# Transformer block on eight cores: LayerNorm sums on ScalarE, four broadcast buffers, seven probability buffers, output stored in halves

## The reference

```python
x = x + attn(_layernorm(x), ...)
x = x + ffn(_layernorm(x), ...)

# attn: 16 query heads of 64, one K and one V head for all
q = jnp.einsum('bnd,hkd->bnhk', r, query_proj)
k = jnp.einsum('bmd,dk->bmk', r, key_proj)
v = jnp.einsum('bmd,dv->bmv', r, value_proj)
sim = jnp.einsum('bnhk,bmk->bnhm', q, k) / jnp.sqrt(64)
o = jnp.einsum('bnhm,bmv->bnhv', softmax(sim), v)
out = jnp.einsum('bnhv,dhv->bnd', o, output_proj)

# ffn: 64 channels, an inner width of 16 for each
s = jnp.einsum('btd,dm->btm', x, Win) + bin_
h = relu(s[..., None] * W1 + b1)
g = jnp.einsum('btmh,mh->btm', h, W2) + b2
out = jnp.einsum('btm,md->btd', g, Wout) + bout
```

## Time and profile before

| | us |
|---|---|
| median of 2 runs | 1667.75 (1655.49 to 1680.01) |
| the profiled execution | 1658.1 |
| its span, slowest core (core 4) | 1656.5 |
| spans of the eight cores | 1645.0 to 1656.5 |
| TensorE busy | 1099.0 (66%) |
| ScalarE busy | 1043.5 (63%) |
| VectorE busy | 472.7 (29%) |
| GpSimd busy | 94.9 (6%) |

### The profile page before, as it was taken

One profiled execution on the slowest core, in us unless ns is written; L12 is line 12 of the kernel. 1 busy time (PEld: TensorE's weight loads), 2 busy tenths in 40 slices (PEclk: granted clock), 3 DMA queues, 4 the chain that ended last, 5 costly groups with the idle time before them and its releaser, 6 DMA issues.

```text
span 1656.5 us, 20837 instructions; the slowest of 8 cores (1645.0 to 1656.5 us)
## 1 busy us (share of the span) xinstructions
PE 1099.0 (66%) x7407; PEld 419.4 (25%) x7424; DVE 472.7 (29%) x759; ACT 1043.5 (63%) x1203; POOL 94.9 (6%) x188
## 2 busy tenths in 40 slices
PE   0366534899999698999789999799997225152420
PEld 0233222333333233333233333233332002020110
DVE  1655676100101110101210101110102036453643
ACT  0211121899999799999799999799998001120201
POOL 0000000000000010000100100100100010000000
PEclk9977755899999899999899999899999658585755
DMA  6211121300000200000200000200000322234232
GB/s 168 101 53 53 53 103 43 104 1 1 1 1 2 66 17 9 12 14 3 66 17 9 16 10 3 66 17 9 17 10 3 116 68 95 84 119 140 78 138 89
DMA packets 27924, 81.75 MB, mean 49 GB/s; under 512 B 9008, under 2 KB 10032, under 8 KB 27568
## 3 DMA queue, kind: packets, MB, share of 16 engines
q1 hardware_dynamic: 19120, 60.87, 11.1%
q0 software_dynamic: 8704, 19.54, 3.6%
HBM read 60.34 MB, written 25.17 MB: 52 GB/s over the span
## 4 chain that ended last, share of the span: by engine, by line
ACT 36%; PE 18%; DMA 17%; DVE 15%; issue 12%; SPq 1%; DVEq 0%; POOLq 0%; ACTq 0%
ACT ptu L496 35%; DMA rcpb<-zscr 4%; DMA zscr<-zscr 4%; DMA big<-x2d 3%; PE qps L334 3%; DMA x2d<-big 3%; PE spa L481 2%; PE oBe L520 2%; PE oAe L520 2%; DVE stats L193 2%; PE spb L481 2%; PE kps L307 2%; DVE g L649 1%; DVE big L676 1%; DVE big L671 1%
## 5 line engine op out<-in xcount | busy, mean ns | idle before, releaser
L496 ACT ACTIVATE ptu<-spb 128x1024 bf16<-128x1024 f32 x512 | 568.5, 1110 | 32.3 <-PE spb L481 31.7
L496 ACT ACTIVATE ptu<-spa 128x1024 bf16<-128x1024 f32 x512 | 569.6, 1112 | 1.5 <-PE spa L481 1.5
L520 PE MATMUL oBo<-ptu,vab 64*65 64x512 bf16 x1024 | 389.8, 381 | 31.7 <-DVE big L535 29.2
L520 PE MATMUL oAo<-ptu,vab 64*65 64x512 bf16 x1024 | 388.5, 380 | 2.5 <-DVE big L535 0.5
L520 PE MATMUL oBe<-ptu,vab 64*65 64x512 bf16 x1024 | 387.3, 378 | 1.4
L520 PE MATMUL oAe<-ptu,vab 64*65 64x512 bf16 x1024 | 385.3, 376 | 1.7
L481 PE MATMUL spb<-qt,k2t 64*128 64x512 bf16 x1024 | 211.5, 384 | 39.0 <-ACT ptu L496 0.9
L481 PE MATMUL spa<-qt,k2t 64*128 64x512 bf16 x1024 | 205.4, 383 | 48.0 <-ACT ptu L496 6.1
L204 ACT ACTIVATE stats<-stats,epsb 128x1 f32<-128x1 f32 x48 | 14.1, 295 | 352.7 <-DVE stats L202 352.7
L535 DVE COPY big<-oBo 65x512 f32<-65x512 f32 x32 | 22.0, 687 | 660.1 <-PE oBo L520 659.8
L222 PE MATMUL trpsA<-identb,r1u 128*128 128x128 bf16 x256 | 32.0, 303 | 165.6 <-DVE r1u L212 165.6
(11 more groups left out here) (60 smaller groups left out, 824.9 us busy)
## 6 DMA issues: line engine op xcount, KB each, us to landing
xbuf<-x_own SPq DMA_DIRECT2D x32, 512.0 KB, 3.3
xbuf<-x_oth SPq DMA_DIRECT2D x16, 512.0 KB, 3.2
rcpb<-zscr POOLq DMA_DIRECT2D x64, 128.0 KB, 2.6
x2d<-big POOLq DMA_DIRECT2D x16, 512.0 KB, 2.9
big<-x2d SPq DMA_DIRECT2D x16, 512.0 KB, 4.2
out<-big SPq DMA_DIRECT2D x16, 512.0 KB, 3.0
xbuf<-wq SPq DMA_DIRECT2D x8, 512.0 KB, 4.5
xbuf<-wp SPq DMA_DIRECT2D x8, 512.0 KB, 4.0
```

The source lines that it names most:

```text
L496: expT[gmc] = S.emit("scalar", lambda s_, gmc=gmc: s_.activation(ptu[:, gmc % 8, :], sp[gmc % 2][:], AF.Exp, scale=0.125), waits=ew, inc=" ...
L520: tgt = S.emit("tensor", lambda te, ob=ob, rg=rg, col=col, mc=mc, gmc=gmc: te.matmul(ob[:], vab[rg:rg + 64, mc, :], ptu[rg:rg + 64, gmc % ...
```

## The change

Five edits.

1. LayerNorm sums, in both parts: `ln_stage1` gives Square an accumulator output for the sum of squares, and adds an Identity activation with an accumulator output for the sum. Both reductions of VectorE go.
2. `rcpb` has four buffers instead of two; each has a semaphore of its own (`zs`, `zs2`, `zs3`, `zs4`). A multiply waits for its own broadcast, a broadcast no longer for the one in front, and four are issued ahead.
3. `ptu` has seven buffers instead of eight (one buffer is 2 KB of each partition, what the two new buffers of `rcpb` take is 4 KB). Exponential `gmc` now waits for `pvT[gmc - 4]` too. `pvT` is set by the matmul with `oi == 3`, the last of the four in a pass, and for gmc-4 that is pass gmc-2.
4. In `emit_D` the reload of tile t waits for the spill of tile t instead of the newest spill, and for the first of the two adds of tile t-2 instead of the second.
5. The output of a tile is stored as two halves of 512 columns by two DMAs with two semaphores.

```diff
-        rcpb = st.enter_context(nc.sbuf_tensor("rcpb", [128, 2, NTW], F32))
+        rcpb = st.enter_context(nc.sbuf_tensor("rcpb", [128, 4, NTW], F32))
-        ptu = st.enter_context(nc.sbuf_tensor("ptu", [128, 8, 1024], BF16))
+        ptu = st.enter_context(nc.sbuf_tensor("ptu", [128, 7, 1024], BF16))
...
         def ln_stage1(li, xt_ap, sc, sq_waits=()):
             dmp = dump(li % 2)
             ln_state["sqa" + str(li)] = S.emit(
-                "scalar", lambda s, a=xt_ap, dmp=dmp: s.activation(dmp, a, AF.Square),
-                waits=list(sq_waits) + [("dve", ln_state["sq2"].get(li - 1, 0))], inc="act")
+                "scalar", lambda s, a=xt_ap, dmp=dmp, c=sc: s.activation(
+                    dmp, a, AF.Square, accum_out=stat(SUMSQ, c)),
+                waits=list(sq_waits) + [("act", ln_state["sq"].get(li - 1, 0))], inc="act")
             ln_state["sq"][li] = S.emit(
-                "vector", lambda v, a=xt_ap, c=sc: v.reduce_sum(stat(SUMS, c), a, axis=AX),
-                waits=[w for w in sq_waits if w[0] != "act"], inc="dve")
+                "scalar", lambda s, a=xt_ap, dmp=dmp, c=sc: s.activation(
+                    dmp, a, AF.Identity, accum_out=stat(SUMS, c)),
+                waits=[("act", ln_state["sqa" + str(li)])], inc="act")
 
         def ln_stage2(li, sc):
-            dmp = dump(li % 2)
-            tsq2 = S.emit("vector", lambda v, c=sc, dmp=dmp: v.reduce_sum(stat(SUMSQ, c), dmp, axis=AX),
-                          waits=[("act", ln_state["sqa" + str(li)])], inc="dve")
-            ln_state["sq2"][li] = tsq2
             S.emit("vector", lambda v, c=sc: v.tensor_scalar_mul(stat(EX2, c), stat(SUMSQ, c), 1.0 / D),
-                   waits=[("dve", tsq2)])
+                   waits=[("act", ln_state["sq"][li])])
...
-            zw = zst["bcT"][max(zst["bcT"])]
-            mw = [("zs", zw), ("dve", tcopyT[k * NHP + i_ // 2])]
+            mw = [(ZS[i_ % 4], zst["bcT"][i_]), ("dve", tcopyT[k * NHP + i_ // 2])]
...
-            if i_ + 2 < HEADS:
-                emit_bcast_ref[0](k, i_ + 2)
+            if i_ + 4 < HEADS:
+                emit_bcast_ref[0](k, i_ + 4)
...
-                ew = [("pe", sPT[gmc])]
+                ew = [("pe", sPT[gmc]), ("pe", pvT.get(gmc - 4, 0))]
...
-                    ptu[:, gmc % 8, :], sp[gmc % 2][:], AF.Exp, scale=0.125),
+                    ptu[:, gmc % 7, :], sp[gmc % 2][:], AF.Exp, scale=0.125),
...
-                            if zst["bcT"]:
-                                bw.append(("zs", zst["bcT"][max(zst["bcT"])]))
-                            if i_ >= 2:
-                                bw.append(("dve", multT[(kk, i_ - 2)]))
+                            if i_ >= 4:
+                                bw.append(("dve", multT[(kk, i_ - 4)]))
...
-                        for i_ in range(2):
+                        for i_ in range(4):
                             emit_bcast(k, i_)
...
-                xw = [("g", spill_t[max(spill_t)]), ("dve", fadd_t.get(t - 2, 0)),
+                xw = [("g", spill_t[t]), ("dve", tfa_t.get(t - 2, 0)),
                       ("dve", multT.get((KL, HEADS - 1), 0))]
...
-                outdma_t[t] = S.emit("sync", lambda e, t=t, q=q: e.dma_start(
-                    out_d.rearrange("(t p) d -> t p d", p=128)[t], obuf(q)),
-                    waits=[("dve", fadd_t[t])], inc=osem, inc_n=16)
+                for h in range(2):
+                    outdma_t[(t, h)] = S.emit("sync", lambda e, t=t, q=q, h=h: e.dma_start(
+                        out_r[t, :, h * 512:(h + 1) * 512], obuf(q)[:, h * 512:(h + 1) * 512]),
+                        waits=[("dve", fadd_t[t])] if h == 0 else (), inc=osems[h], inc_n=16)
```

More of the change, by code:

```diff
@@ L25 @@
 ENGS = ("sync", "tensor", "vector", "scalar", "gpsimd")
-SEMS = ("pe", "dve", "act", "xa", "xb", "xc", "xd", "g", "zg", "zs", "out", "ou2", "wd", "od", "zh", "pl", "x2r")
+SEMS = ("pe", "dve", "act", "xa", "xb", "xc", "xd", "g", "zg", "zs", "zs2", "zs3", "zs4", "out", "ou2", "ou3", "ou4", "wd", "od", "zh", "pl", "x2r")
 DMA_SEMS = {"xa", "xb", "g", "zg", "zs", "out"}
@@ L448, in emit_zmult @@
                 odma_fin[k] = zst["odmaT"]
+        ZS = ("zs", "zs2", "zs3", "zs4")
         emit_bcast_ref = [None]
@@ L520, in build_nc @@
                 tgt = S.emit("tensor", lambda te, ob=ob, rg=rg, col=col, mc=mc, gmc=gmc: te.matmul(
-                    ob[:], vab[rg:rg + 64, mc, :], ptu[rg:rg + 64, gmc % 8, col:col + 512],
+                    ob[:], vab[rg:rg + 64, mc, :], ptu[rg:rg + 64, gmc % 7, col:col + 512],
                     start=(mc == 0), stop=(mc == MC - 1)),
@@ L564, in build_nc @@
                         if k > 0 and (k - 1) in zstate:
-                            rw.append(("zs", zstate[k - 1]["bcT"][15]))
-                            tzw.append(("zs", zstate[k - 1]["bcT"][15]))
+                            for s_ in range(4):
+                                rw.append((ZS[s_], zstate[k - 1]["bcT"][12 + s_]))
+                                tzw.append((ZS[s_], zstate[k - 1]["bcT"][12 + s_]))
                         trec = S.emit("vector", lambda v: v.reciprocal(recipz[:], zstage[:]),
@@ L583, in emit_bcast @@
                             bw = [("zh", tzo)]
[L584 to L587 removed]
+                            if i_ >= 4:
+                                bw.append(("dve", multT[(kk, i_ - 4)]))
                             else:
[L589 removed]
+                                bw.append(("dve", multT.get((kk - 1, 12 + i_), 0)))
                             zst["bcT"][i_] = S.emit("gpsimd", lambda e, i_=i_: e.dma_start(
[L591 removed]
+                                rcpb[0:64, i_ % 4, :],
                                 zscr.rearrange("c h n -> h c n")[i_]),
[L593 removed]
+                                waits=bw, inc=ZS[i_ % 4], inc_n=16)
                         emit_bcast_ref[0] = emit_bcast
[L596 removed]
+                        for i_ in range(4):
                             emit_bcast(k, i_)
@@ L619, in build_nc @@
         r2evac_t = {}
+        tfa_t = {}
+        out_r = out_d.rearrange("(t p) d -> t p d", p=128)
         spill_t = {}
@@ L664, in emit_D @@
                 sm = "wd" if t % 2 == 0 else "x2r"
-                osem = "out" if t % 2 == 0 else "ou2"
-                xw = [("g", spill_t[max(spill_t)]), ("dve", fadd_t.get(t - 2, 0)),
+                osems = ("out", "ou3") if t % 2 == 0 else ("ou2", "ou4")
+                xw = [("g", spill_t[t]), ("dve", tfa_t.get(t - 2, 0)),
                       ("dve", multT.get((KL, HEADS - 1), 0))]
@@ L672, in emit_D @@
                     obuf(q), x2dbuf(q), fo[:], op=ALU.add),
-                    waits=[("pe", fo_mm_t[t]), (sm, txl), (osem, outdma_t.get(t - 2, 0)),
+                    waits=[("pe", fo_mm_t[t]), (sm, txl),
+                           (osems[0], outdma_t.get((t - 2, 0), 0)),
+                           (osems[1], outdma_t.get((t - 2, 1), 0)),
                            ("dve", multT.get((KL, HEADS - 1), 0))],
                     inc="dve")
+                tfa_t[t] = tfa
                 fadd_t[t] = S.emit("vector", lambda v, q=q: v.tensor_tensor(
@@ L761, in build_nc @@
                 waits=S.barrier_waits("gpsimd"), inc="g", inc_n=16)
-        S.emit("gpsimd", lambda e: e.nop(), waits=[("out", outdma_t[14]), ("ou2", outdma_t[15])])
+        S.emit("gpsimd", lambda e: e.nop(), waits=[
+            ("out", outdma_t[(14, 0)]), ("ou3", outdma_t[(14, 1)]),
+            ("ou2", outdma_t[(15, 0)]), ("ou4", outdma_t[(15, 1)])])
         S.flush()
```

2 lines of the change are left out of this document (1 added, 1 removed).

## The result

The changed kernel takes 1695.9 us (median of 9 runs, 1691.5 to 1697.4), the kernel before 1656.95 (median of 8 runs). The ratio is 1.0237, with a 95% interval of 1.0223 to 1.0251: slower. The forecast was 1701, within 1664 to 1738. Ratios leave out runs in a slower state, in which the cores of one die show a lower granted clock (1677 at 0.75 instead of 0.86 in one run of the kernel before); here these are two of the eight before, 1679 and 1680.

A forecast was written before the change was run, and what follows sets the result against it. ScalarE's exponentials were taken to set attention's pace, a chain of short waits the last part's. First part -29, attention +113, last part -41 give +43 on a span of 1656.5; with 1.6 around it 1701 us, range 1664 to 1738.

The forecast's parts named there:

- The exponential's wait: Attention: exponentials wait for the pass's last PV matmul, 2.10 us for two instead of 1.83; +147 before the stalls' 34 go.
- The boundary's 0.5 a head pair: Attention, between head pairs: TensorE's remaining stall on PSUM copies adds 0.5 us a pair, making 34.1.
- The three stalls: Attention, near the start of query tiles 1 to 3: ScalarE stalls of about 11.3 us each go, 34 in all.
- First part: LayerNorm of 32 tiles with K, V, Q products: a tile step falls from 4.46 to 3.9 us, -29 in all.
- the ring that was argued: First part: Ln waits for VectorE's small operations, these for the Identity in front; 3.61 us, 3.9 with the sum outputs.
- Last part: Normalizing, projection and feed-forward: multiplies -30, LayerNorm -16, feed-forward +5, together -41 us.
- The multiplies: Last part, sixteen normalizing multiplies: broadcasts leave the ring, the copy through r1u sets 4.2 us for two; -30.
- The feed-forward groups: Last part: the second half store adds an issue of 0.34 us before reloads and the last store, about +5.
- The first: Rival: same mechanism but smaller, a head pair of 33.75 would be inside the 2% band; time 1680, chance 0.32.
- The second: Rival: attention not slower, the wait is met in passing because the last PV matmul finishes earlier; 1568, chance 0.07 (under 1650).
- the third: Rival: TensorE's clock falls to 1.2 GHz in attention through idle gaps, +430, time 2130; chance 0.03.
- The fourth: Rival: Identity needs table loads, two per tile in the first part, +82, time 1783; chance 0.01.

The follow-up runs named there:

- e2: The kernel before, with eight ptu buffers, plus only the exponential's wait for the last PV matmul of pass n-2: 1789.1 us, ratio 1.078.
- e3: The changed kernel, but the exponential waits for the first of the four PV matmuls of pass n-2, not the last: 1589.5 us, ratio 0.958.
- e8: The changed kernel with each pass's four PV matmuls put in front of its score product in TensorE's queue: 1568.7 us, ratio 0.943.
- e5: The kernel before with only the four rcpb buffers and their semaphores; eight ptu buffers stay, the eighth in r1t: 1623.8 us, ratio 0.977.
- e10: The changed kernel with ln_stage2(step - 1) written behind ln_stage1(step) in the first part's loop instead of in front: 1668.4 us, ratio 1.0045.
- e9: e8 with the x2d reload ahead of the stores and a semaphore for each half of r1u: 1514.3 us, ratio 0.911.
- e6: The kernel before with only the weaker waits of the reload and the two half stores: 1663.8 us, ratio 1.0028.
- e1: The changed kernel with an eighth ptu buffer (in r1t) and without the exponential's wait for PV matmuls: 1573.1 us, ratio 0.949.
- e7: e1 with the x2d reload of tile t+1 issued before the stores of tile t in SyncE's queue: 1526.1 us, ratio 0.919.

## Why the prediction was right

The slowest core's span went from 1656.5 to 1692.8, +36 for the +43 of the sum. Its three terms missed by 3 (first part), 3 (attention) and 1 (last part), all to the faster side.

**The exponential's wait** carried it. Foreseen: exponential 0.93 behind the product, 2.10 for two, 34.1 a head pair, attention +113. Measured: 0.91, 2.08, 34.03, +110. e2 shows that the wait alone makes it, e3 and e8 that its size is the place of the release in TensorE's queue. The boundary's 0.5 a head pair, called the weakest term, is 34.03 - 16 x 2.09 = 0.6, with the 2.09 that most rounds take.

**The three stalls** are gone in the changed kernel, as foreseen: past the first ten, no exponential on the slowest core starts more than 1.5 us behind the one in front of it. At the old pace four broadcasts shorten them by 5 to 6 and not by 7 each (e5).

**First part**: -29 foreseen, -32 measured. The step is 3.98 for 3.9. Each sum output is an instruction of its own of 0.19 (the rows of the LayerNorm step above), and Square to Identity is 1.22, where 1.04 + 0.15 + 0.10 was assumed, and the small operations take 1.01 to the Ln (124.87 to 125.88) for 0.83. The -32 is that of the two slowest cores; all eight lie at 290 to 296 before and 259 to 265 after, 31 apart in the mean. Most of the miss is in the stretch from a slab's last copy to the next product: counted from the copy's end it was 18.3 to 18.7 and is 13.9 to 14.1, so six times 4.5 less where 4.1 was foreseen. The single row of 18.4 that the prediction took was one of the short ones. e10 shows the ring that was argued.

**Last part**: -41 foreseen, -42 measured on the slowest cores and -41 in the mean of the eight, and that it fits to 1 us is partly luck. The multiplies gained 28 in the mean (68.4 to 40.4) and 26 on the slowest cores, for 30. On the slowest core after, from the first broadcast to the last multiply's end

```profile
1382.82 2.07 POOL L587 DMA_DIRECT2D rcpb<-zscr  x4 [24.72 <-DMA zscr<-zscr]
...
1397.88 0.69 DVE L432 TENSOR_TENSOR r1u<-big,rcpb 64x512 bf16<-64x512 f32 x1 [7.83 <-DMA ot<-r1u]
...
1423.75 0.69 DVE L432 TENSOR_TENSOR r1u<-big,rcpb 64x512 bf16<-64x512 f32 x1 [2.66 <-DMA ot<-r1u]
```

it is 41.6 and not 37.3. The first copy through `r1u` was issued 0.9 behind the first of four loads of `x_own`, took 7.3 to land where the median is 2.3, and held VectorE 7.8 us; 3 had been allowed for these loads. That the loads slowed it is argued from this and not shown by a run. The copy is what the odd multiplies wait for, as foreseen, and e9 took most of that wait out. The LayerNorm steps gained 15 in the mean for 16: an undisturbed one gained 1.3 (6.12 instead of 7.45), but not all of the 13 are. The feed-forward groups, for which +5 was foreseen, are only 1.7 longer in the mean (101.7 for 100.0), and not longer on the slowest cores. In e6, where the stores were changed alone, they are 4.5 longer. So the multiplies' shortfall was met by stores that cost less here than alone, and why they did is open.

**Rivals.** The first (inside 2%) missed by little: the ratio's interval begins at 1.022, and a head pair of 34.03 lies 0.3 above the 33.75 that it needed. The second is ruled out by e1 and e2. For the third the granted clock in attention is 1.00, with a recorded idle of 0.35 in every second pass. (The 0.27 of the prediction counts a pass as three starts 0.21 apart; by the recorded ends the gap before was 0.09, from 695.50 to 695.59 in the earlier trace rows.) The gate did not swing here, so the rule of the Trainium skill on short idles did not bear on this loop ("TensorE: Matmul & The Clock Gate", second failure mode). The fourth: two table loads with LayerNorm, as before, with 48 Identities in the program:

```profile
L185 ACT ACT_TABLE_LOAD x2 | 2.6, 1283 | 98.0 <-DVE ot L432 55.1
```

and so the trace agrees with the Trainium skill's "ScalarE: Activation LUTs", which counts identity among the fillers of every set.

## What to carry to other kernels

Before an engine at the bound gets a wait for a buffer, look where in the releasing queue the released instruction stands: a wait for something that stands behind the producer of the same pass puts all that lies between into the loop, and costs what then exceeds the engine's own pace (1.66, 1.85 and 2.08 here, against 1.83). Putting it ahead of the producer made the wait free, with one buffer less. A mean duration that falls (1.11 to 1.02) can be lost overlap and not speed. In an in-order queue a weaker wait freed nothing until the instruction's place was moved too (e7, 47 us). Moving whole passes over the data from one engine to another is worth what the ring through both allows; look for that ring before choosing the order of emission (e10, 27 us for three moved lines).

## What the runs showed of the hardware that was not expected

A ScalarE activation with a sum output appears as two records, the activation and `ACTIVATION_READ_ACCUMULATOR` of 0.18 to 0.19 us, and the next activation that waits for it starts 1.22 us behind its start for 128x1024. Behind two half stores of 256 KB the transfer queued next on SyncE is issued 0.91 us after the first, behind one whole store 0.38, with no gain in when it lands: the reload of 512 KB takes 4.0 from its issue to land in e6 and the changed kernel and 4.6 in e1, and 4.2 behind whole stores. With TensorE idle 0.35 us by the records in every second pass of 1.04, the granted clock of attention stayed at 1.00, the higher of the two levels.
